# A graph network's edge sums: GpSimd instead of VectorE makes the one-hot tiles

## The chip, the cores and the metric

The kernel runs on one core of one Trainium2 chip. The metric is the time on the device in microseconds of one launch. Engines are called TensorE (PE), VectorE (DVE), ScalarE (ACT), GpSimd (POOL) and SyncE (SP, which here only issues DMAs); SBUF is the on-chip memory of 128 partitions, PSUM the accumulation memory ("pb" in the rows).

## The reference

Four graph layers over 6250 nodes of 128 features, each followed by a layer norm of the residual. The 206250 edges are sorted by destination. The change touches the first layer alone:

```
xw  = x @ W                          # 6250 x 128
ew  = edge_attr @ edge_w             # one row of 128 for each edge
msg = xw[src] * ew
out = segment_sum(msg, dst) + b      # each edge's message added to its destination's row
x   = layernorm(x + out)
# layers 1 to 3: the same edges, with weights that depend only on src and dst
```

## The kernel before

At the start TensorE makes xw and SP stores it to a table in HBM ("xw"). Then comes a loop, unrolled, of NH = 202 steps, one for each 1024 edges (8 tiles of 128 edges, one edge in each partition; the last step has 4 tiles, so 1612 tiles in all). In a step n

- GpSimd issues one indirect DMA for each tile (line 722), which fetches the 128 rows xw[src] into `gath`, a ring of NG = 4 steps. A ring slot is free when the products of step n-4 are done (`s_msg`, line 716). Before the fifth gather of a step (from step 7 on) GpSimd waits for TensorE too (line 721's event): `s_pe >= n`, which is window n-2 done, and `s_amm >= 2 (n-6)`, the dense-adjacency products of step n-2 done. In 25 of the steps it issues one more indirect DMA for the slots of a pair of node blocks (line 705).
- TensorE has made the edge products ew (line 1326) in two PSUM banks; VectorE multiplies them with the gathered rows into `msg` (two instructions, line 909).
- VectorE makes `hot_win`, eight one-hot tiles of 128 edges x 64 nodes in one instruction (line 802, 128 x 512): element (edge, j) is 1 where the edge's destination, counted from the step's first destination, is j. It makes them one step ahead, those of step n+1 in step n; two sets take turns.
- TensorE makes the edge products of step n+1 and then sums the eight tiles' msg^T x hot_win in PSUM (line 1405, the "window"). VectorE adds the window to the sums yT in the following step (line 849).
- Beside this, the step builds a dense adjacency piece for the later layers: one-hot tiles on VectorE (lines 835 and 837), products on TensorE (line 1378), evicted by ScalarE (line 1636), stored by SP (line 618), summed for degrees (line 1384). A "job" of the first layers' norm or of the second layer's sums follows (line 1368 and others).

After the loop the other layers run on dense adjacency chunks read back from HBM; GpSimd has no gathers there. The order on each engine is that of the program; semaphores are the only link. The names in the rows: `big` is the SBUF room that holds gath, msg, hot_win, rel and more; `pb` is PSUM; `tmp` holds the staging tiles. `cols` (columns' numbers) lies in PSUM, `cols_pf` holds the same numbers in SBUF; `rel` is each edge's destination relative to its step's first.

Of the kernel before, what the change touches and what calls it, by code (L numbers as in the profile page):

```python
# [16 lines left out]
ALU = mybir.AluOpType  # L17
# [7 lines left out]
P = 128  # L25
NB = -(-N // P)
NP = NB * P
T8 = 8
SN = 32
NH = 2 * max(-(-E // (2 * T8 * P)), NP // (2 * SN) + 1)  # L30
NI = NH // 2
T = NH * T8
WIN = 64
# [14 lines left out]
LAG = 5  # L48
# [81 lines left out]
def build(nc, xT_d, x_d, ea_d, src_d, dst_d, next_d, edges_d, firstq_d, first16_d, half_d, w_d, vec_d, out_d):  # L130
    ctx = ExitStack()
    with ctx:
# [40 lines left out]
        hot_win = part([P, 2 * T8, WIN], F32)  # L173
# [9 lines left out]
        rel = part([P, T], F32)  # L183
# [70 lines left out]
        cols_pf = sb("cols_pf", [P, P])  # L254
# [17 lines left out]
        cols = PB[:, 7, 0:P + KW]  # L272

        s_in = {n: sem("in_" + n) for n in ("w0", "w", "edge_w", "xT0", "xT1", "xT2", "xT3", "vecs", "src", "edges", "firsts", "rows", "x")}
        s_const = sem("consts_made")
        s_rowxw, s_rowev = sem("xw_mm"), sem("xw_evac")
        s_rowst = [sem(f"xw_stored{h}") for h in range(4)]
        s_tab = sem("dve_table_step")
# [10 lines left out]
        s_seen = sem("wait_over")  # L289
        s_ea = [sem(f"ea_in{h}") for h in range(NG)]  # L290
        s_pe = sem("window_and_next_ew_done")
        s_msg = sem("msg_done")
        s_hotw = sem("hot_win_done")
        s_add = sem("yT_added")
        s_hot = sem("hot_ready")
        s_amm = sem("a_mm")
# [379 lines left out]
        def _(pool):  # L676
# [21 lines left out]
            def slots_in(b):  # L698
                if b == 0:
                    pool.wait_ge(s_firstin, 16)  # L700
                    pool.sem_inc(s_seen, 1)
                if b >= 2:
                    pool.wait_ge(s_prep, b - 1)
                    pool.sem_inc(s_seen, 1)
                nc.gpsimd.indirect_dma_start(slots[:, b % 2, :, :].rearrange("p e k -> p (e k)"), None, edges_d,
                                             bass.IndirectOffsetOnAxis(ap=first_edge[:, b:b + 1], axis=0)).then_inc(s_slot[b % 2], 16)

            pool.wait_ge(s_in["src"], 16)
            pool.wait_ge(s_rowxw, 2 * NT)
            for h in range(4):  # L710
# [2 lines left out]
            for n in range(NH):  # L713
                if n >= NG:
                    pool.wait_ge(s_msg, 2 * (n - NG) + 2)
                    pool.sem_inc(s_seen, 1)
                for t in range(n * T8, min(n * T8 + T8, ET)):
                    if t % T8 == T8 // 2 and n >= LAG + 2:
                        pool.wait_ge(s_pe, n)
                        pool.wait_ge(s_amm, 2 * (n - LAG - 1))  # L720
                        pool.sem_inc(s_seen, 1)
                    nc.gpsimd.indirect_dma_start(gath[:, T8 * (n % NG) + t % T8, :], None, xw_d,  # L722
                                                 bass.IndirectOffsetOnAxis(ap=src_i[:, t:t + 1], axis=0)).then_inc(s_gath[n % NG], 16)
                if n == 0:
                    slots_in(0)
                if n % BL == BL // 2 and n // BL + 1 < NPB:
                    slots_in(n // BL + 1)
            for q in range(NCH):
                here = y[:, CB * q:min(CB * q + CB, NB), :]
                pool.wait_ge(s_w2["xs"], q + 1)  # L730
                nc.gpsimd.tensor_tensor(here, here, vecs[:, B_L2, :].unsqueeze(1).broadcast_to([P, min(CB, NB - CB * q), D]), ALU.add).then_inc(s_w2["yb"], 1)
# [12 lines left out]
            for q in range(NCH - 1):  # L744
# [3 lines left out]
                for h in range(0, CB, 2):  # L748
                    last = nc.gpsimd.tensor_tensor(off_pivot[:, h:h + 2, :], rows_q[:, h:h + 2, :], x[:, 0:2, :], ALU.subtract)  # L749
# [18 lines left out]
        def _(v):  # L768
# [27 lines left out]
            nc.vector.tensor_copy(cols[:, 0:P], cols_pf[:, :])  # L796
            nc.vector.tensor_copy(cols[:, P:P + KW], cols_key[:, :]).then_inc(s_tab, 1)
            v.wait_ge(s_tab, 4)

            def window_hot(n):  # L800
                at_tile = T8 * (n % 2)
                nc.vector.tensor_tensor(hot_win[:, at_tile:at_tile + T8, :], cols[:, 0:WIN].unsqueeze(1).broadcast_to([P, T8, WIN]),  # L802
                                        rel[:, n * T8:n * T8 + T8].unsqueeze(2).broadcast_to([P, T8, WIN]), ALU.is_equal).then_inc(s_hotw, 1)

            cuts = [NPB + 1]

# [94 lines left out]
                    v.wait_ge(s_fhi, g + 1)  # L901
                    nc.vector.scalar_tensor_tensor(out=group(parts_v[1], g), in0=xn_g, scalar=SCALE, in1=group(parts_v[0], g), op0=ALU.mult, op1=ALU.subtract).then_inc(s_part, 1)

            window_hot(0)
            for n in range(NH):
                v.wait_ge(s_pe, n + 1)
                v.wait_ge(s_gath[n % NG], 16 * T8 * (n // NG) + 16 * min(T8, ET - n * T8))
                for q in range(2):
                    nc.vector.tensor_tensor(msg[:, T8 * (n % 2) + 4 * q:T8 * (n % 2) + 4 * q + 4, :], PB[:, q, :].rearrange("p (t f) -> p t f", f=D),  # L909
                                            gath[:, T8 * (n % NG) + 4 * q:T8 * (n % NG) + 4 * q + 4, :], ALU.mult).then_inc(s_msg, 1)  # L910
                if n + 1 < NH:
                    window_hot(n + 1)
                if n > 0:
                    window_add(n - 1)
                job_out(n - 2)
                fold_shift(n)
                if n % BL == 2 and n // BL < NPB:
                    split_slots(n // BL)
                if 0 <= n + 1 - LAG < NA:
                    hots(n + 1 - LAG)  # L920
                fold_stats(n)
                if n == 5:
                    for g in range(NG1):
                        nc.vector.tensor_scalar(flags[:, 3 + g:4 + g], half_i[:, STEP_OF[g]:STEP_OF[g] + 1], float(GB * P * (g + 1)), None, ALU.is_lt)
                        here = win_tab[0:1, STEP_OF[g]:STEP_OF[g + 1] if g + 1 < NG1 else NH]
                        last = nc.vector.tensor_scalar(here, here, float(GB * P * (g + 1)), None, ALU.max)
                    last.then_inc(s_off, 1)
                elif n == 6:
                    v.wait_ge(s_in["rows"], 16)
                    nc.vector.tensor_tensor(less, next_i, dst_i, ALU.is_lt).then_inc(s_off, 1)  # L930
                elif n == 7:
                    v.wait_ge(s_off, 2)
                    nc.vector.tensor_scalar(less, less, 0.0, None, ALU.is_gt, ALU.add, accum_out=flags[:, 1:2]).then_inc(s_off, 1)
                elif n == 8:
                    v.wait_ge(s_off, 3)
                    nc.vector.scalar_tensor_tensor(out=less, in0=dst_i, scalar=float(N), in1=rel[:, 0:T], op0=ALU.is_lt, op1=ALU.mult).then_inc(s_off, 1)
                elif n == 9:
                    v.wait_ge(s_off, 4)
                    nc.vector.tensor_scalar(less, less, float(WIN), None, ALU.is_ge, ALU.add, accum_out=flags[:, 0:1]).then_inc(s_off, 1)
                elif n == BL * (NPB - 1) + 4:  # L940
                    nc.vector.tensor_tensor(pair_deg[:, :, :], below[:, :, 1:3], below[:, :, 0:2], ALU.subtract).then_inc(s_deg["pairs"], 1)
                    nc.vector.tensor_scalar(unused[:, 0, 0:NPB], below[:, :, 2], float(P), None, ALU.is_ge, ALU.add, accum_out=flags[:, 2:3]).then_inc(s_off, 1)
# [6 lines left out]
            for b in range(NL):  # L949
                last = nc.vector.bn_stats(stats[:, 1, b, :], x[:, LB + b, :])  # L950
            last.then_inc(s_lx, 1)
            v.wait_ge(s_lx, 2)
            for b in range(NL):
                last = nc.vector.bn_aggr(mean_var[:, LB + b, :], stats[:, 1, b, :])
# [133 lines left out]
            with v.If(g_off > 0):  # L1088
# [5 lines left out]
                for t in range(NT):  # L1094
# [4 lines left out]
                    for q, nb in ((0, 4), (1, BT - 4)):  # L1099
                        last = nc.vector.tensor_copy(xnT[:, 4 * q:4 * q + nb, :], PB[:, 2 + q, 0:nb * P].rearrange("p (b f) -> p b f", f=D))  # L1100
# [4 lines left out]
                    for q, nb in ((0, 4), (1, BT - 4)):  # L1105
                        last = nc.vector.tensor_tensor(x[:, t * BT + 4 * q:t * BT + 4 * q + nb, :], xn[0][:, 4 * q:4 * q + nb, :], PB[:, 4 + q, 0:nb * P].rearrange("p (b f) -> p b f", f=D), ALU.add)
# [22 lines left out]
            for j in range(NCH):  # L1129
                nb, here = width(j), slice(CB * j, min(CB * j + CB, NB))  # L1130
                v.wait_ge(S["lin"], j + 1)
                for b in range(nb):
                    row = y[:, CB * j + b, :]
                    last = nc.vector.scalar_tensor_tensor(out=row, in0=PB[:, 4 + j % 2, b * P:b * P + P], scalar=on_l2[:, CB * j + b:CB * j + b + 1], in1=row, op0=ALU.mult, op1=ALU.add)
                last.then_inc(S["y"], 1)
                v.wait_ge(S["y"], j + 1)
                for b in range(nb):
                    last = nc.vector.bn_stats(stats[:, j % 2, b, :], y[:, CB * j + b, :])
                last.then_inc(S["stats"], 1)
                v.wait_ge(S["stats"], 2 * j + 1)  # L1140
                for b in range(nb):
                    last = nc.vector.bn_aggr(mean_var[:, CB * j + b, :], stats[:, j % 2, b, :])
# [101 lines left out]
            for h, rows_of in enumerate((low_rows[:, :], float(NB // 2))):  # L1244
                last = nc.vector.scalar_tensor_tensor(out=lane_rows[:, h, :], in0=x[:, h, :], scalar=rows_of, in1=sum_1[:, h, :], op0=ALU.mult, op1=ALU.add)
# [6 lines left out]
            for h, rows_of in enumerate((low_rows[:, :], float(NB // 2))):  # L1252
                last = nc.vector.scalar_tensor_tensor(out=twice_1[:, h, :], in0=lane_rows[:, h, :], scalar=rows_of, in1=twice_1[:, h, :], op0=ALU.mult, op1=ALU.subtract)
# [19 lines left out]
            for t in range(NT + 2):  # L1273
# [4 lines left out]
                if 1 <= t <= NT:  # L1278
                    v.wait_ge(s_bn_sum, t)
                    for b in range(BT):  # L1280
                        last = nc.vector.bn_stats(stats[:, t % 2, b, :], x[:, (t - 1) * BT + b, :])
# [4 lines left out]
                if t < NT:  # L1286
# [5 lines left out]
                    for q, (b0, b1) in enumerate(((0, 4), (4, BT))):  # L1292
                        here = x[:, t * BT + b0:t * BT + b1, :]
                        last = nc.vector.tensor_tensor(here, here, PB[:, 2 + 2 * (t % 3) + q, 0:(b1 - b0) * D].rearrange("p (b f) -> p b f", f=D), ALU.add)
                    last.then_inc(s_bn_sum, 1)
                if 1 <= t <= NT:
                    v.wait_ge(s_bn, stats_at)
                    for b in range(BT):
                        last = nc.vector.bn_aggr(mean_var[:, (t - 1) * BT + b, :], stats[:, t % 2, b, :])
                    aggr_at.append(bn_at(last))  # L1300
            v.wait_ge(s_bn, shift_at[NT - 1])
            for b in range(NB - BT, NB):
                last = nc.vector.tensor_scalar(x[:, b, :], x[:, b, :], rstd[:, b:b + 1], shift[:, b:b + 1], ALU.mult, ALU.add)
# [578 lines left out]
```

## Time and profile before

| | |
|---|---|
| time, median of 3 runs | 2831.36 us (2830.82 to 2834.81) |
| profiled execution, its span | 3281.4 us |
| the page gives no other time of the profiled execution | |
| busy in the span: PE, DVE, POOL, ACT | 2326.1, 1559.3, 1652.8, 497.8 us |
| first and last gather of the loop start at | 32.38 and 2520.00 us |
| gathers in the loop (lines 722 and 705) | 1612 + 25 |

The span is from the first to the last instruction of one profiled execution; it is 450 us longer than the median of the runs that were timed without a profile. In the rows, "idle before <-X" is the time that the engine stood still ahead of an instruction and what ended it; "issue" means that nothing the profile shows was waited for, "remote" that the releaser could not be named. A gather's duration on GpSimd is the time to write its descriptors, not the transfer.

### The profile page before, as it was taken

Reading aid. Unit: us, or ns where it says so; the run is one execution under the profiler, and the core shown is the slowest. Engines: PE = TensorE matmul, PEld = TensorE weight load, DVE = VectorE, ACT = ScalarE, POOL = GpSimd, SP = SyncE. Lnnn points to the kernel's source line nnn. Section 1 sums busy time; section 2 is a strip of 40 time slices with the busy share of each in tenths; the row PEclk is TensorE's granted clock in tenths of the full one; section 3 lists DMA queues with packets and bytes.
Section 4 is the critical chain, followed back from the end, with each engine's and each line's share of the span. In section 5 each row is a group of like instructions: output and inputs, shape, how many; then the busy total and the mean of one; then the engine's idle time right before and its main releaser. Section 6 shows DMA issues by size and latency. Waiting matters only on the chain.

```text
span 3281.4 us, 35388 instructions
## 1 busy us (share of the span) xinstructions
PE 2326.1 (71%) x13074; PEld 1466.3 (45%) x13074; DVE 1559.3 (48%) x2576; ACT 497.8 (15%) x798; POOL 1652.8 (50%) x1762
## 2 busy tenths in 40 slices
PE   3566656666666666667666567666677989999996
PEld 2344444444444444444444344444444544455553
DVE  2555554555554555555555555555554531222126
ACT  1011111111111111111111111111111221111113
POOL 5566656656666666656666656656664110002212
PEclk6556556566666776777777777777777999999998
DMA  6223232323333343433344344444445988876661
GB/s 203 57 86 87 82 88 84 106 84 92 107 96 99 101 122 95 120 100 110 113 135 114 106 116 121 136 121 132 119 128 120 245 294 306 291 268 247 248 242 40
DMA packets 456700, 456.22 MB, mean 139 GB/s; under 512 B 163573, under 2 KB 402250, under 8 KB 456522
## 3 DMA queue, kind: packets, MB, share of 16 engines
q1 hardware_dynamic: 237358, 281.24, 25.7%
q0 software_dynamic: 52832, 109.16, 12.5%
q10 hardware_dynamic: 166332, 63.48, 8.0%
q8 instruction: 108, 1.77, 0.2%
q14 instruction: 70, 0.57, 0.1%
HBM read 368.61 MB, written 85.13 MB: 138 GB/s over the span
## 4 chain that ended last, share of the span: by engine, by line
another core or an unknown queue 46%; PE 35%; ACT 7%; issue 7%; DVE 2%; DMA 2%; SPq 0%; ACTq 0%; POOL 0%; DVEq 0%; POOLq 0%
PE pb L1509 8%; PE pb L1510 8%; ACT tmp L1636 7%; PE pb L1378 5%; PE pb L1405 4%; PE pb L1368 2%; PE pb L1384 2%; PE pb L1326 2%; PE pb L1437 2%; PE pb L1527 1%; DMA big<-at 1%; DMA tmp<-at 0%; ACTq L1642 0%; ACT big L1670 0%
## 5 line engine op out<-in xcount | busy, mean ns | idle before, releaser
L722 POOL DMA_INDIRECT big<-xw,big x1612 | 1527.1, 947 | 954.7 <-issue 580.0
L909 DVE TENSOR_TENSOR big<-pb,big 128x512 f32<-128x512 f32 x404 | 260.0, 685 | 1073.1 <-remote 683.2
L1378 PE MATMUL pb<-big 128*128 128x98 f16 x3136 | 272.9, 248 | 643.2 <-ACT tmp L1636 562.1
L1405 PEld LDWEIGHTS pb<-big 128*128 128x128 f32 x3232 | 546.2, 258 | 349.1 <-issue 334.1
L1405 PE MATMUL pb<-big 128*128 128x64 f32 x3232 | 584.1, 346 | 124.4 <-issue 119.6
L1636 ACT CAST tmp<-pb 128x784 f16<-128x784 f32 x392 | 318.3, 812 | 2043.0 <-remote 1628.5
L1378 PEld LDWEIGHTS pb<-big 128*128 128x128 f16 x3136 | 231.9, 124 | 726.5 <-issue 405.6
L835 DVE TENSOR_TENSOR big<-pb,big 128x2048 f16<-128x2048 f32 x196 | 447.5, 2283 | 0.8
L1326 PE MATMUL pb<-big 64*128 64x512 f32 x808 | 327.3, 898 | 108.4 <-DVE big L909 83.7
L837 DVE TENSOR_TENSOR big<-pb,big 128x1568 f16<-128x1568 f32 x196 | 348.8, 1780 | 0.0
L1384 PE MATMUL pb<-tmp,ident 128*128 128x392 f16 x784 | 239.1, 446 | 0.0
L1509 PE MATMUL pb<-big,x 128*128 128x512 f16 (+1 forms) x637 | 230.3, 369 | 6.6 <-issue 6.6
L1509 PE MATMUL pb<-big,yT 128*128 128x512 f16 (+1 forms) x637 | 230.7, 369 | 3.6 <-DMA big<-at 3.6
L1510 PE MATMUL pb<-big,yT 128*128 128x512 f16 (+1 forms) x637 | 230.5, 369 | 0.0
L1510 PE MATMUL pb<-big,x 128*128 128x512 f16 (+1 forms) x637 | 230.1, 369 | 0.0
L1368 PE MATMUL pb<-big,yT 128*128 128x448 f16 x804 | 199.3, 399 | 9.2 <-issue 9.0
L1326 PEld LDWEIGHTS pb<-big 64*128 64x128 f32 x808 | 83.6, 253 | 135.2 <-DVE big L909 90.2
L749 POOL TENSOR_TENSOR wts<-x 128x256 f32<-128x256 f32 x24 | 16.9, 724 | 246.9 <-DVE x L1206 246.9
L1368 PEld LDWEIGHTS pb<-big,yT 128*128 128x128 f16 x804 | 87.9, 110 | 111.2 <-issue 60.0
L802 DVE TENSOR_TENSOR big<-pb,big 128x512 f32<-128x512 f32 x202 | 137.5, 681 | 0.0
L737 POOL MEMSET vecs<- 128x256 f32 x1 | 0.3, 312 | 271.4 <-DVE yT L1153 271.4
L1384 PEld LDWEIGHTS pb<-tmp,ident 128*128 128x128 f16 x784 | 87.6, 126 | 51.5 <-issue 40.2
(231 smaller groups left out, 1600.0 us busy)
## 6 DMA issues: line engine op xcount, KB each, us to landing
at<-tmp SPq DMA_DIRECT2D x196, 392.0 KB
big<-at SPq DMA_DIRECT2D x24, 3200.0 KB, 10.9
big<-at SPq DMA_DIRECT2D x24, 3072.0 KB, 19.7
big<-at ACTq DMA_DIRECT2D x32, 896.0 KB
big<-xw,big POOLq DMA_INDIRECT x1612
big<-in_ea SPq DMA_DIRECT2D x202, 64.0 KB
big<-at SPq DMA_DIRECT2D x13, 896.0 KB
big<-at ACTq DMA_DIRECT2D x24, 336.0 KB
```

The source lines that it names most:

```text
L722: nc.gpsimd.indirect_dma_start(gath[:, T8 * (n % NG) + t % T8, :], None, xw_d, bass.IndirectOffsetOnAxis(ap=src_i[:, t:t + 1], axis=0)).th ...
L835: nc.vector.tensor_tensor(hot_lo[:, at_pair:at_pair + NPR, :], cols[:, 0:P].unsqueeze(1).broadcast_to([P, NPR, P]), lokeyT[:, b % 3, c:c + ...
L837: last = nc.vector.tensor_tensor(hot_key[:, at_pair:at_pair + NPR, :], cols[:, P:P + KW].unsqueeze(1).broadcast_to([P, NPR, KW]), lokeyT[: ...
L909: nc.vector.tensor_tensor(msg[:, T8 * (n % 2) + 4 * q:T8 * (n % 2) + 4 * q + 4, :], PB[:, q, :].rearrange("p (t f) -> p t f", f=D), gath[: ...
L1326: last = nc.tensor.matmul(PB[:, q, :], ea[4 * ED * q:4 * ED * q + 4 * ED, n % NG, :], edge_w[4 * ED * q:4 * ED * q + 4 * ED, 4 * q:4 * q + ...
L1368: nc.tensor.matmul(bank, parts_v[part_of][:, b0 + b, :], a_piece[:, :, b, :], start=(b == 0 and part_of == 0), stop=(b == size - 1 and par ...
L1378: last = nc.tensor.matmul(PB[:, 4 + g, i * KW:i * KW + KW], hot_lo[:, at_pair, :], hot_key[:, at_pair, :], start=True, stop=True)
L1384: last = nc.tensor.matmul(PB[:, 6, 0:NB * T8], ident16[:, :], stage[:, j % 2, :].rearrange("p (h d) -> p h d", d=SN)[:, :, g * T8:g * T8 + ...
L1405: last = nc.tensor.matmul(PB[:, 2 + n % 2, 0:WIN], msg[:, T8 * (n % 2) + t, :], hot_win[:, T8 * (n % 2) + t, :], start=(t == 0), stop=(t = ...
L1509: nc.tensor.matmul(PB[:, c, 0:n], hi[:, b, :], piece, start=(b == 0), stop=False)
L1510: last = nc.tensor.matmul(PB[:, c, 0:n], lo[:, b, :], piece, start=False, stop=(k == 2 and b == NB - 1))
L1636: nc.scalar.copy(stage[:, j % 2, :].rearrange("p (h d) -> p h d", d=SN)[:, :, c:c + 4 * GP].rearrange("p h (k i a) -> p h k i a", k=2, a=2 ...
```

## The change

GpSimd makes the one-hot tiles, eight instructions of 128 x 64 for each step (one for each tile, with the edge's relative destination as a scalar of each partition, and `cols_pf` in SBUF as the numbers), behind the step's gathers. VectorE's instruction of 128 x 512 goes. GpSimd's wait before the fifth gather goes; the new instructions wait for `s_pe >= n`, that is for window n-2, which read the set they overwrite.

```diff
+            def window_hot(n):
+                if n >= 2:
+                    pool.wait_ge(s_pe, n)
+                for t in range(T8):
+                    last = nc.gpsimd.tensor_scalar(hot_win[:, T8 * (n % 2) + t, :], cols_pf[:, 0:WIN], rel[:, n * T8 + t:n * T8 + t + 1], None, ALU.is_equal)
+                last.then_inc(s_hotw, 1)
...
                 for t in range(n * T8, min(n * T8 + T8, ET)):
-                    if t % T8 == T8 // 2 and n >= LAG + 2:
-                        pool.wait_ge(s_pe, n)
-                        pool.wait_ge(s_amm, 2 * (n - LAG - 1))
-                        pool.sem_inc(s_seen, 1)
                     nc.gpsimd.indirect_dma_start(gath[:, T8 * (n % NG) + t % T8, :], None, xw_d,
                                                  bass.IndirectOffsetOnAxis(ap=src_i[:, t:t + 1], axis=0)).then_inc(s_gath[n % NG], 16)
                 if n == 0:
                     slots_in(0)
+                    pool.wait_ge(s_tab, 2)
+                    pool.wait_ge(s_const, 3)
                 if n % BL == BL // 2 and n // BL + 1 < NPB:
                     slots_in(n // BL + 1)
+                window_hot(n)
...
-            def window_hot(n):
-                at_tile = T8 * (n % 2)
-                nc.vector.tensor_tensor(hot_win[:, at_tile:at_tile + T8, :], cols[:, 0:WIN].unsqueeze(1).broadcast_to([P, T8, WIN]),
-                                        rel[:, n * T8:n * T8 + T8].unsqueeze(2).broadcast_to([P, T8, WIN]), ALU.is_equal).then_inc(s_hotw, 1)
...
-            window_hot(0)
             for n in range(NH):
...
-                if n + 1 < NH:
-                    window_hot(n + 1)
```

On GpSimd, in the middle of the loop, two steps stand in the order before as follows (`msg_done` is `s_msg`, `window_and_next_ew_done` is `s_pe`, `a_mm` is `s_amm`; DMA rows are the gathers):

```order
L722 DMA big<-xw,big 128x128 [waits msg_done]
L722 DMA big<-xw,big 128x128 x3
L722 DMA big<-xw,big 128x128 [waits window_and_next_ew_done,a_mm]
L722 DMA big<-xw,big 128x128 x3
L722 DMA big<-xw,big 128x128 [waits msg_done]
L722 DMA big<-xw,big 128x128 x3
```

The same place after the change:

```order
L725 DMA big<-xw,big 128x128 [waits msg_done]
L725 DMA big<-xw,big 128x128 x7
L712 TENSOR_SCALAR big<-cols_pf,big 128x64 [waits window_and_next_ew_done]
L712 TENSOR_SCALAR big<-cols_pf,big 128x64 x7
L725 DMA big<-xw,big 128x128 [waits msg_done]
L725 DMA big<-xw,big 128x128 x7
```

The wait inside the eight gathers is gone, and eight compute instructions stand between one step's gathers and the next step's.

On VectorE, one step of the loop before (the L909 rows are the products with the gathered rows, L802 the one-hot tiles, L849 the window's addition, L835 and L837 the adjacency's one-hot tiles):

```order
L909 TENSOR_TENSOR big<-pb,big 128x512 [waits gathered3,window_and_next_ew_done]
L909 TENSOR_TENSOR big<-pb,big 128x512
L802 TENSOR_TENSOR big<-pb,big 128x512
L844 TENSOR_LOAD big
L844 ISA x2
L849 ISA [waits yT_added,window_and_next_ew_done]
L849 TENSOR_TENSOR yT<-yT,pb 128x64
L835 TENSOR_TENSOR big<-pb,big 128x2048 [waits lokeyT_ready,a_mm]
L837 TENSOR_TENSOR big<-pb,big 128x1568
```

And after the change:

```order
L909 TENSOR_TENSOR big<-pb,big 128x512 [waits gathered3,window_and_next_ew_done]
L909 TENSOR_TENSOR big<-pb,big 128x512
L845 TENSOR_LOAD big
L845 ISA x2
L850 ISA [waits yT_added,window_and_next_ew_done]
L850 TENSOR_TENSOR yT<-yT,pb 128x64
L836 TENSOR_TENSOR big<-pb,big 128x2048 [waits lokeyT_ready,a_mm]
L838 TENSOR_TENSOR big<-pb,big 128x1568
```

One instruction has gone from each step; the rest stands as it stood.

## Rows read from the trace of the kernel before

**Rows 1.** The page: span, and each engine's busy time, share and instructions.

```profile
span 3281.4 us, 35388 instructions
PE 2326.1 (71%) x13074; PEld 1466.3 (45%) x13074; DVE 1559.3 (48%) x2576; ACT 497.8 (15%) x798; POOL 1652.8 (50%) x1762
```

**Rows 2.** Two stretches: from, to, length, engines' busy time (count), PEclk, DMA share, GB/s.

```profile
32.00:2521.00 2489.00, 1605.22 (x9228) 1076.01 (x9229) 1311.58 (x1774) 353.29 (x489) 1550.81 (x1637) 0.69 0.38 107
2521.00:3281.00 760.00, 704.89 (x3744) 375.88 (x3743) 229.58 (x740) 135.95 (x293) 97.58 (x106) 0.96 0.71 238
```

**Rows 3.** GpSimd's order of time at the loop's start: start, duration, instruction, idle before.

```profile
32.38 0.96 POOL L722 DMA_INDIRECT big<-xw,big  x1 [24.59 <-issue]
33.64 0.95 POOL L722 DMA_INDIRECT big<-xw,big  x1 [0.30 <-issue]
```

**Rows 4.** The same at the loop's end: the last two gathers.

```profile
2518.75 0.95 POOL L722 DMA_INDIRECT big<-xw,big  x1 [0.31 <-issue]
2520.00 0.95 POOL L722 DMA_INDIRECT big<-xw,big  x1 [0.30 <-issue]
```

**Rows 5.** GpSimd's groups by form: count, busy us, mean ns, idle before.

```profile
L722 POOL DMA_INDIRECT big<-xw,big x1612 | 1527.1, 947 | 954.7 <-issue 580.0 <-PE pb L1378 266.3 <-remote 95.0
L705 POOL DMA_INDIRECT big<-in_edges,first_edge x25 | 23.7, 948 | 7.6 <-issue 7.6
L749 POOL TENSOR_TENSOR wts<-x 128x256 f32<-128x256 f32 x24 | 16.9, 724 | 246.9 <-DVE x L1206 246.9
L739 POOL TENSOR_SCALAR valid<-valid 128x1 f32<-128x1 f32 x1 | 0.2, 233 | 0.0
L741 POOL TENSOR_SCALAR low_rows<-valid 128x1 f32<-128x1 f32 x1 | 0.2, 218 | 0.1
```

**Rows 6.** GpSimd in order of time, two steps in the middle of the loop.

```profile
1227.20 0.95 POOL L722 DMA_INDIRECT big<-xw,big  x1 [3.33 <-PE pb L1378]
1228.45 0.95 POOL L722 DMA_INDIRECT big<-xw,big  x1 [0.30 <-issue]
...
1235.96 0.95 POOL L722 DMA_INDIRECT big<-xw,big  x1 [0.30 <-issue]
1237.85 0.95 POOL L722 DMA_INDIRECT big<-xw,big  x1 [0.95 <-issue]
```

**Rows 7.** TensorE, then ScalarE, in order of time at that place.

```profile
1231.15 0.52 PE L1378 MATMUL pb<-big 128*128 128x98 f16 x8
1232.17 2.05 PE L1368 MATMUL pb<-big,yT 128*128 128x448 f16 x10
1238.07 0.67 PE L1378 MATMUL pb<-big 128*128 128x98 f16 x8 [3.84 <-ACT tmp L1636]
...
1237.11 0.81 ACT L1636 CAST tmp<-pb 128x784 f16<-128x784 f32 x1 [7.88 <-remote]
```

**Rows 8.** VectorE's groups between 600 and 2300 us, columns as in rows 5.

```profile
L835 DVE TENSOR_TENSOR big<-pb,big 128x2048 f16<-128x2048 f32 x138 | 315.1, 2283 | 0.6
L909 DVE TENSOR_TENSOR big<-pb,big 128x512 f32<-128x512 f32 x274 | 176.4, 686 | 694.2 <-remote 439.0 <-DMA big<-xw,big 157.2 <-PE pb L1405 84.4
L802 DVE TENSOR_TENSOR big<-pb,big 128x512 f32<-128x512 f32 x137 | 93.3, 681 | 0.0
```

**Rows 9.** GpSimd's order of time where it computes, behind the loop.

```profile
2915.47 0.31 POOL L737 MEMSET vecs<- 128x256 f32 x1 [271.38 <-DVE yT L1153]
2915.72 0.31 POOL L738 MEMSET tmp<- 128x256 f32 x1
...
2955.67 1.30 POOL L749 TENSOR_TENSOR wts<-x 128x256 f32<-128x256 f32 x2 [39.14 <-DVE x L1206]
```

**Rows 10.** VectorE's order of time before the loop: the table of relative destinations, the first one-hots.

```profile
26.91 1.83 DVE L791 TENSOR_TENSOR big<-big 128x1616 f32<-128x1616 int32 x1
29.27 0.69 DVE L802 TENSOR_TENSOR big<-pb,big 128x512 f32<-128x512 f32 x1
```

## The prediction

> **What bounds the kernel now.** I read the page's head first: 3281.4 us of span, no engine busy for more than 71% of it, GpSimd for 50% [rows 1]. A mean over such a span hides its stages, so I cut it at the last gather. Up to there (2489 us) GpSimd's gathers take 1551 us and TensorE is busy for 1605 us at a mean granted clock of 0.69, a mix of its two levels 1.2 and 2.4 GHz; behind it (760 us) TensorE is busy for 705 us at 0.96 and GpSimd for 98 [rows 2]. The second stage is TensorE's, and the change doesn't touch it. The question is what bounds the first.
>
> Gathers start 1.25 us apart wherever nothing is waited for, 0.95 us of it busy and 0.30 idle [rows 3, 4, 6]. That pace is the same directly after a pause of 3.33 us (1227.20 to 1228.45) as in the middle of a run [rows 6]. A queue that is drained at a fixed rate would let the first gathers after a pause come faster; so the pace belongs to GpSimd itself. There are 1612 + 25 gathers [rows 5], and 1636 intervals of 1.251 us (0.947 + 0.304) are 2047 us. From the first gather at 32.38 the last could start at 2079; it starts at 2520.00 [rows 3, 4]. So the profiled execution has 441 us of waits on GpSimd's queue. GpSimd's group says the same: 954.7 us idle, less 24.6 before the first and 1611 times 0.304, leaves 440 [rows 3, 5]. By name most of it ends with TensorE's L1378 (266.3 us), or is unnamed [rows 5]; in two steps in the middle it is 3.33 and 0.65 us ahead of the fifth gather, the place of the wait that the change removes [rows 6].
>
> Now the time without a profile: 2831.36, that is 450 us less than the span. TensorE's stage behind the loop is 93% busy and can't give that back (its idle time is 55 us) [rows 2]. The 450 must come out of the loop, and the loop holds 441 us of waits above the pure pace of the gathers. Head 32.4, gathers 2047.6 and the rest from 2521 on, 760.4, make 2840.4, and the kernel takes 2831. So in a timed run GpSimd gathers practically without a pause. I take it that the profile slows what stands behind those waits: TensorE's eight L1378 matmuls end at 1231.67 by the records and ScalarE, which needs them, starts at 1237.11, 5.4 us later, with nothing else shown between [rows 7]. In a timed run that lag is not there, or not so long. **Forecast: the loop is bound by GpSimd's queue**, whose step is (2831.4 - 32.4 - 760.4) / 202 = 10.09 us, against 8 x 1.251 plus 25 x 1.251 / 202 = 10.16.
>
> **The change, part by part.**
>
> *VectorE loses L802*: 202 times 0.681 us [rows 8]. In the loop VectorE is busy 1312 of 2489 us [rows 2], 6.5 us a step against a step of 10.09. It waits for gathers and TensorE, not they for it. Worth nothing to the time (the other end: if the chain ran through VectorE, 138 us; its 694 us of idle ahead of L909 alone between 600 and 2300 us [rows 8] exclude that).
>
> *The mid-step wait goes*: in the profile 441 us of the span at most, less what reappears elsewhere; in a timed run nothing, since the time is already 9 us below the sum without waits (2840.4). What would take its place is the new wait for window n-2. GpSimd meets it after eight gathers rather than four, so it is half a step (5 us) later for the same count, and the part on `s_amm` is dropped. The step itself becomes 12.3 us (below), and window n-2 is wanted only a full step after its one-hots were made. I count 0 in a timed run and 0 to 40 us in the profile. Behind this wait stand the next step's gathers, and VectorE's products behind these.
>
> *GpSimd gains 202 x 8 = 1616 instructions of 128 x 64.* No row shows one. From below: the element rate of a memset, 256 elements in 0.25 us from start to start [rows 9], gives 0.06 us for 64. From above: a tensor_tensor of 256 elements with two inputs, 1.30 us for two, so 0.58 from start to start [rows 9]; one input and a quarter of the elements can hardly take more. Nearest: tensor_scalar of one element, 0.233 for a comparison and 0.218 for an addition [rows 5]. To 0.22 come 63 elements at about 1 ns (0.06), and from start to start a memset shows 0.06 less than its duration (0.31 against 0.25 [rows 9]): 0.22 to 0.23. The scalar here is read from SBUF for each partition, where those rows had a constant; I add 0.045 for that and take 0.27. Eight: 2.16 us. The passage from gather to compute and back may cost up to the 0.30 idle that each gather has ahead of it, or hide it; I take 0.04. **2.2 us a step, 444 us in 202 steps.** The bounds are 8 x 0.06 x 202 = 97 and (8 x 0.58 + 0.30) x 202 = 998.
>
> By the Trainium skill (GPSIMD Engine Reference, "Performance pitfalls for Q7 kernels" and "Performance versus the Vector engine") each small read command costs about 102 cycles at 1.2 GHz, not overlapped, and a one-input body 1.03 to 2.03 cycles an element. Two reads (tile and scalar) and 64 elements would be 0.22 to 0.28 us, an estimate from that page, and the time 3195 to 3284. No row here has the same instruction; the one-element rows lie beside it. The skill also warns (Perfetto Trace Analysis, on GpSimd's boundaries) that a GpSimd span should be timed from start to start, as is done above. And it rules that elementwise work belongs on VectorE, since GpSimd dispatches in software: one instruction of 0.68 us there against eight here is that rule in numbers.
>
> None of this lies beside other work: GpSimd's queue is in order, and gathers of step n+1 stand behind the one-hots of step n. The slot wait (`s_msg`) allows gathers four steps ahead, so there is always a gather ready to be issued, and each 2.2 us is 2.2 us lost to them.
>
> *Start*: rel is written at 28.74 and VectorE's first one-hots start at 29.27 [rows 10], before the first gather at 32.38 [rows 3]: the two new waits of step 0 cost nothing.
>
> **Sum.** Profiled: 3281.4 - 441 + 444 = 3285, the same as before within its doubt. Timed: the waits are not in the median, so 2831.4 + 444 = **3275 us**. TensorE has room: 1605 us at 0.69 of full clock is 7.9 us a step, and if all of it ran at the lower level (0.5) it would be 11.0, below the new step of 12.3 [rows 2].
>
> **The rivals.**
>
> *A. The gathers are faster without a profile, and the loop is bound by TensorE's chain through the mid-step wait.* Then the 0.30 idle is the profiler's, eight gathers take 7.6 us, and the one-hots fit into a step of 10.09: 7.6 + 2.2 = 9.8. With the wait gone GpSimd runs ahead, gathered rows are never late, and the step falls to that 9.8: 202 x 0.29 = 59 us, 2772 us. It decides at a gather pace of (10.09 - 2.2) / 8 = 0.99 us; below it the change is faster, at 1.05 us it costs 0.5 x 202 = 101 us and gives 2930. For it: the profile's slowness has to come from somewhere, and instructions that report are candidates. Against it: the pace without waits meets the timed loop to 0.07 us a step, which would be chance; and memsets follow each other without any idle time [rows 9]. I give faster 5%, and up to 3100 by a faster gather pace 6% more.
>
> *B. The one-hots are cheap*, 0.15 us or less each, because the cores that don't write descriptors work ahead and only the dispatch counts: 1.2 us a step, 242 us, 3074. Against it the 0.22 of one element [rows 5]. 6%.
>
> *C. They are dear*, 0.45 us or more each: the read of the scalar, the comparison or a stop at each passage from descriptor work to compute. 3.9 us a step, 788 us, 3619. For it: tensor_tensor's 0.58 [rows 9]; against it, the one-element rows. 10%.
>
> *D. TensorE becomes a second bound*: with longer steps it idles more, its clock is granted at the lower level throughout, and in steps with the longest jobs it needs more than 12.3 us. Its mean of 11.0 leaves 1.3 us; if a third of the steps overran by 1.5 us, 100 us more, 3375. 8%, inside the range.
>
> *E. The change does not move the time at all*, the gathers being limited by something that drains behind GpSimd so that one-hots hide in its idle time: 2831. The pace after a pause speaks against it. 3%.
>
> **How the numbers follow.** The forecast with its sizes between 0.19 and 0.42 us an instruction (1.5 to 3.4 us a step, 3140 to 3520) has 62%; D 8%; A 11%; B 6%; C 10%; E 3%. Range 3110 to 3520: it leaves out A and E, most of B and nearly all of C, about 2 in 10. What a measurement of this kernel can tell from no change is about 0.2%, 6 us. Faster 5% (A), same 3% (E), slower 92%.
>
> **What the profile after would show.** Right: a span near 3280, about the same as before, while the time is 400 us longer; start to start of the new instructions near 0.27; GpSimd's idle ahead of gathers near 0.30 each with few waits named; some 12.3 us from one step's first gather to the next. Wrong, if gathers or one-hots wait for TensorE as long as before, if the instruction takes 0.1 or 0.5, or if the time moves by less than 150 us, which would say that a timed gather is shorter than a profiled one.

## The result and the profile after

| | before | after |
|---|---|---|
| time, median | 2832.74 us (4 runs) | 3496.78 us (4 runs) |
| ratio to before | 1 | 1.2339 (95% interval 1.2322 to 1.2357) |
| span of the profiled execution | 3281.4 us | 3493.1 us |

The change costs 664 us, 3.29 us for each of the 202 steps. The forecast was 444 us, 2.2 us a step; the time lies inside the range (3110 to 3520), near its upper end. Ratios and their intervals, here and below, are estimated from the runs of both kernels; the quotient of two medians differs from them by about 0.001.

The page after, its span and busy times, which answer to [rows 1]:

```profile
span 3493.1 us, 36609 instructions
PE 2530.8 (72%) x13074; PEld 1638.9 (47%) x13074; DVE 1443.4 (41%) x2374; ACT 498.4 (14%) x798; POOL 2342.9 (67%) x3378
```

GpSimd has 1616 instructions and 690 us of busy time more, VectorE 202 instructions and 116 us less (202 times 0.68 would be 138; where the other 22 us went is not traced, and nothing below depends on it). The two stages, cut at the last instruction of the loop's queue, answer to [rows 2] (columns as there):

```profile
32.00:2746.00 2714.00, 1819.37 (x9297) 1252.94 (x9298) 1199.45 (x1578) 356.56 (x493) 2238.08 (x3247) 0.65 0.34 98
2746.00:3493.00 747.00, 693.96 (x3677) 370.15 (x3674) 226.49 (x734) 133.29 (x290) 100.08 (x113) 0.97 0.72 242
```

The profiled execution that [rows 2] show was itself 450 us longer than the kernel's time, so its loop can't be set against this one. A second profile of the kernel before (the last experiment below) has a span of 2829.5 us, which fits the time. Its two stages:

```profile
32.00:2080.00 2048.00, 1566.02 (x9252) 1080.00 (x9253) 1316.11 (x1779) 355.43 (x491) 1548.10 (x1637) 0.73 0.46 130
2080.00:2829.00 749.00, 697.34 (x3722) 372.48 (x3720) 226.27 (x734) 134.29 (x291) 97.46 (x106) 0.97 0.72 241
```

The second stage is what it was (749 and 747 us). The first grew from 2048 to 2714 us, by 666: all of the loss is there. GpSimd's groups by form, which answer to [rows 5]:

```profile
L725 POOL DMA_INDIRECT big<-xw,big x1612 | 1542.0, 957 | 485.5 <-issue 485.5
L712 POOL TENSOR_SCALAR big<-cols_pf,big 128x64 f32<-128x64 f32 x1616 | 675.4, 437 | 6.6
L705 POOL DMA_INDIRECT big<-in_edges,first_edge x25 | 23.6, 946 | 7.6 <-issue 7.6
```

All of the gathers' idle time is now "issue": no wait is named. (24 of the 485.5 us stand before the first gather.) The one-hots take 0.437 us each and 675 us in all by their durations, about the 664 us of the result; neighbours overlap a little, so the sum of durations is slightly too high. One step of GpSimd in order of time, in the middle of the loop (start, duration, instruction, idle before), beside [rows 6]:

```profile
1203.07 0.94 POOL L725 DMA_INDIRECT big<-xw,big  x1 [0.30 <-issue]
1204.05 3.34 POOL L712 TENSOR_SCALAR big<-cols_pf,big 128x64 f32<-128x64 f32 x8
1207.55 1.03 POOL L725 DMA_INDIRECT big<-xw,big  x1 [0.16 <-issue]
1208.89 0.94 POOL L725 DMA_INDIRECT big<-xw,big  x1 [0.30 <-issue]
...
1217.34 3.34 POOL L712 TENSOR_SCALAR big<-cols_pf,big 128x64 f32<-128x64 f32 x8
```

From block to block it is 13.29 us. From the start of the eighth gather to that of the next step's first it is 4.48 us instead of 1.25, and the second gather follows 1.34 us behind the first instead of 1.25, because the first takes 1.03 us there and not 0.94: 3.3 us in all for the block. What the other engines do meanwhile shows in the waits (waiter, releaser, us in total, times, longest):

```profile
ACT tmp L1634 <- PE pb L1376: 2262.7, 373, 26.6
DVE big L909 <- DMA big<-xw,big: 1476.4, 201, 18.7
PEld pb L1324 <- DVE big L909: 926.4, 195, 19.9
POOL big L725 <- issue: 485.5, 1612, 23.9
```

VectorE waits for the gathers' data in 201 of 202 steps, 7.3 us a step; TensorE waits for VectorE, ScalarE for TensorE. In the loop GpSimd names no wait for another engine. The chain of waits that ended last says it in one line: POOL 64% of the span, 44% in L725 and 19% in L712.

The one-hots take as long beside a busy VectorE as beside an idle one. The last of each block of eight took 0.433 us in the mean in the 147 steps in which VectorE computed throughout, and 0.430 us in 33 steps in which it stood still. So their price is not a contest with VectorE.

### The profile page after: what moved, and what is told of

Same layout as the page of the kernel before. It is cut to its first block, busy times and chain, and to the rows that moved or that the text cites. A ratio compares the mean times of both kernels' runs of the same rounds, so it can differ in the third digit from the quotient of the medians.

```text
span 3493.1 us, 36609 instructions
## 1 busy us (share of the span) xinstructions
PE 2530.8 (72%) x13074; PEld 1638.9 (47%) x13074; DVE 1443.4 (41%) x2374; ACT 498.4 (14%) x798; POOL 2342.9 (67%) x3378
## 4 chain that ended last, share of the span: by engine, by line
POOL 64%; PE 18%; issue 14%; DMA 2%; DVE 1%; SPq 0%; ACT 0%; POOLq 0%; ACTq 0%; DVEq 0%
POOL big L725 44%; POOL big L712 19%; PE pb L1507 7%; PE pb L1508 7%; PE pb L1435 1%; DMA big<-at 1%; POOL big L705 1%; PE pb L1525 1%; DMA tmp<-at 0%; PE pb L1542 0%; PE pb L1558 0%; DMA xw<-big 0%; DVE stats L1279 0%; DVE x L1292 0%; PE pb L1446 0%
## 5 line engine op out<-in xcount | busy, mean ns | idle before, releaser
L725 POOL DMA_INDIRECT big<-xw,big x1612 | 1542.0, 957 | 485.5 <-issue 485.5
L1324 PE MATMUL pb<-big 64*128 64x512 f32 x808 | 374.3, 1020 | 894.1 <-DVE big L909 891.4
L909 DVE TENSOR_TENSOR big<-pb,big 128x512 f32<-128x512 f32 x404 | 260.3, 686 | 1477.7 <-DMA big<-xw,big 1476.4
L1403 PEld LDWEIGHTS pb<-big 128*128 128x128 f32 x3232 | 663.5, 313 | 272.3 <-issue 236.2
L1403 PE MATMUL pb<-big 128*128 128x64 f32 x3232 | 700.4, 406 | 3.5 <-DVE big L909 2.4
L712 POOL TENSOR_SCALAR big<-cols_pf,big 128x64 f32<-128x64 f32 x1616 | 675.4, 437 | 6.6
L1376 PEld LDWEIGHTS pb<-big 128*128 128x128 f16 x3136 | 276.0, 135 | 40.3 <-issue 18.0
L1376 PE MATMUL pb<-big 128*128 128x98 f16 x3136 | 289.7, 256 | 3.4 <-DVE big L838 2.3
L1382 PE MATMUL pb<-tmp,ident 128*128 128x392 f16 x784 | 280.6, 510 | 0.0
L1382 PEld LDWEIGHTS pb<-tmp,ident 128*128 128x128 f16 x784 | 99.6, 143 | 64.7 <-issue 61.9
```

The lines of the kernel that those rows point to most:

```text
L712: last = nc.gpsimd.tensor_scalar(hot_win[:, T8 * (n % 2) + t, :], cols_pf[:, 0:WIN], rel[:, n * T8 + t:n * T8 + t + 1], None, ALU.is_equal)
L1324: last = nc.tensor.matmul(PB[:, q, :], ea[4 * ED * q:4 * ED * q + 4 * ED, n % NG, :], edge_w[4 * ED * q:4 * ED * q + 4 * ED, 4 * q:4 * q + ...
L1376: last = nc.tensor.matmul(PB[:, 4 + g, i * KW:i * KW + KW], hot_lo[:, at_pair, :], hot_key[:, at_pair, :], start=True, stop=True)
L1382: last = nc.tensor.matmul(PB[:, 6, 0:NB * T8], ident16[:, :], stage[:, j % 2, :].rearrange("p (h d) -> p h d", d=SN)[:, :, g * T8:g * T8 + ...
L1403: last = nc.tensor.matmul(PB[:, 2 + n % 2, 0:WIN], msg[:, T8 * (n % 2) + t, :], hot_win[:, T8 * (n % 2) + t, :], start=(t == 0), stop=(t = ...
```

## The experiments

The theory: the loop lasts as long as GpSimd's in-order queue, a gather is 1.25 us of it, and each one-hot instruction adds its own time. Each experiment's expectation names the rivals that it tells apart. Five of them don't compute the layer's sums, since they leave out gathers, all or half of the one-hots, or the scalar that the one-hots compare with; they tell only of the time.

### The wait alone removed

```diff
-                    if t % T8 == T8 // 2 and n >= LAG + 2:
-                        pool.wait_ge(s_pe, n)
-                        pool.wait_ge(s_amm, 2 * (n - LAG - 1))
-                        pool.sem_inc(s_seen, 1)
```

> Only GpSimd's mid-step wait is removed; VectorE keeps the one-hots. Theory (GpSimd's queue is saturated in a timed run and the wait costs nothing there): time 2832 us within 0.3%, while the profiled span falls from 3281 to about 2840, since the 441 us of waits were the profile's. Rival (the wait holds the timed loop back, gathers being faster than 1.25 us without a profile): the time falls by 1% or more, below 2805.

Measured: 2833.51 us, ratio 1.0001 (0.9991 to 1.0010); span 2830.9. Of GpSimd's waits in that profile, the gathers' is this; two more rows name VectorE, 16 times, for at most 0.3 us each:

```profile
POOL big L718 <- issue: 510.6, 1596, 24.5
```

The wait costs nothing. The last gather starts at 2077.96 us, where the sum of pure gathers had put it (2079). The interval excludes the rival's gain of 1%.

### The one-hots alone moved

The changed kernel with the four lines above put back.

> Only the one-hots are moved to GpSimd; the mid-step wait stays. Theory: the time is that of the full change, 3497 us within 0.3%, because with a step of 13.3 us TensorE is always ahead of the wait. Rival (the wait's removal gave something back in the full change): slower than 3497 by 20 us or more.

Measured: 3497.86 us, ratio to before 1.2346 (1.2326 to 1.2367), the change's own being 1.2339. The removed wait gives nothing back; the whole cost is the one-hots'.

### One gather of eight left out

```diff
-                for t in range(n * T8, min(n * T8 + T8, ET)):
+                for t in [t for t in range(n * T8, min(n * T8 + T8, ET)) if t % T8 not in (6,)]:
...
-                v.wait_ge(s_gath[n % NG], 16 * T8 * (n // NG) + 16 * min(T8, ET - n * T8))
+                v.wait_ge(s_gath[n % NG], 16 * 7 * (n // NG) + 16 * min(7, ET - n * T8))
```

> The kernel before, but the seventh of a step's eight gathers is left out (201 gathers fewer, the products use what lies in the buffer). Theory: each gather is 1.25 us of the time, so 201 x 1.251 = 251 us less, 2581 us, if TensorE's and VectorE's chain allows a step of 8.8 us. Rival (a step of 10.09 us is TensorE's chain, gathers are hidden): 2832 within 1%. Rival (a timed gather is 1.0 us): 2632.

Measured: 2584.16 us, ratio 0.9124 (0.9109 to 0.9139), so 248 us less by the ratio and 251 by the medians, for 201 gathers: 1.23 to 1.25 us each. This is the price of one gather measured in timed runs, and it is the pace of the profile. The 0.30 us of idle ahead of each gather is real time, not the profiler's.

### Three gathers of eight left out

The same edit with `(1, 5, 6)`, and 5 in place of 7 (3 in the last step).

> The kernel before with the second, sixth and seventh gathers of each step left out (604 fewer). It shows the bound that lies under GpSimd's. Theory: GpSimd's queue alone would give 2832 - 604 x 1.251 = 2076 us; I expect the chain through TensorE and VectorE (7 to 9 us a step) to end first, so 2250 to 2600. Rival (TensorE already bounds a step of 10.09): 2832 within 1%.

Measured: 2190.81 us, ratio 0.7741 (0.7721 to 0.7760). Below the range I had written: the chain under GpSimd's bound is faster than I took it for. The loop's stretch, and GpSimd's longest named wait in it:

```profile
32.00:1426.00 1394.00, 1226.86 (x9210) 853.23 (x9210) 1295.20 (x1768) 354.62 (x490) 975.37 (x1033) 0.90 0.57 162
```

```profile
POOL big L722 <- PE pb L1378: 133.0, 106, 6.2
```

A step is 1394 / 202 = 6.9 us, and the mid-step wait on L1378 now does bite (133 us, 0.3 us of idle ahead of each of the 106 gathers included). VectorE is busy for 1295 of the 1394 us (93%). That doesn't make it the next bound: GpSimd's 1033 gathers, 1.25 us apart, fill 1291 us (93%) as well. The two aren't told apart here, and whether taking 0.68 us a step off VectorE would pay at this pace wasn't tried. TensorE was busy for 1227 us at a granted clock of 0.90, where nearly the same matmuls (9210 and 9297 in the two stretches) took it 1819 us at 0.65 in the changed kernel. So its busy time in the changed kernel doesn't say how much time it needs.

### VectorE's relief without its price

The kernel before; the one-hot buffer is zeroed once, VectorE's instruction is left out and nothing comes in its place, so the windows' sums are zeros.

```diff
+            nc.gpsimd.memset(hot_win[:, :, :], 0.0).then_inc(s_hotw, 1)
...
-            window_hot(0)
...
-                if n + 1 < NH:
-                    window_hot(n + 1)
...
-                pe.wait_ge(s_hotw, n + 1)
+                pe.wait_ge(s_hotw, 1)
```

> The kernel before without any one-hot tiles for the windows (their buffer is zeroed once, VectorE's instruction of 128 x 512 goes, nothing is added to GpSimd). It is the change's relief of VectorE without its price. Theory (VectorE is not on the path of the loop): 2833 us within 0.2%. Rival (VectorE's 0.68 us a step is worth something that the change's price covered up): 2700 to 2825 us.

Measured: 2833.53 us, ratio 0.9994 (0.9985 to 1.0004). The relief is worth nothing here.

### A constant for the scalar

```diff
-                    last = nc.gpsimd.tensor_scalar(hot_win[:, T8 * (n % 2) + t, :], cols_pf[:, 0:WIN], rel[:, n * T8 + t:n * T8 + t + 1], None, ALU.is_equal)
+                    last = nc.gpsimd.tensor_scalar(hot_win[:, T8 * (n % 2) + t, :], cols_pf[:, 0:WIN], float(t), None, ALU.is_equal)
```

> The changed kernel with a constant in place of the scalar of each partition (the one-hot tiles hold the wrong columns). Theory S (the read of the scalar made the instruction 0.41 us where 0.27 was forecast): start to start falls to 0.23 to 0.30 and the time by 1616 x 0.11 to 0.18, to 3205 to 3320 us. Theory E (it is the comparison's cost for each element or a fixed cost): start to start stays at 0.41 and the time at 3497.

Measured: 3468.27 us, ratio 1.2236 (1.2216 to 1.2257), 28.5 us less than the change: 0.018 us an instruction. GpSimd's group:

```profile
L712 POOL TENSOR_SCALAR big<-cols_pf 128x64 f32<-128x64 f32 x1616 | 575.2, 373 | 54.8
```

Theory S falls: 0.018, not 0.11 to 0.18. Start to start became uneven (mostly 0.33 to 0.43, 0.39 in the mean), which is why a duration of 0.373 instead of 0.437 bought so little: the idle time ahead of the one-hots rose from 6.6 to 54.8 us, and that ahead of the gathers from 485.5 to 507.7.

### Half of the columns

```diff
-                    last = nc.gpsimd.tensor_scalar(hot_win[:, T8 * (n % 2) + t, :], cols_pf[:, 0:WIN], rel[:, n * T8 + t:n * T8 + t + 1], None, ALU.is_equal)
+                    last = nc.gpsimd.tensor_scalar(hot_win[:, T8 * (n % 2) + t, 0:WIN // 2], cols_pf[:, 0:WIN // 2], rel[:, n * T8 + t:n * T8 + t + 1], None, ALU.is_equal)
...
+            nc.gpsimd.memset(hot_win[:, :, :], 0.0).then_inc(s_const, 1)
```

The other halves are zeroed once ahead of the loop.

> The changed kernel with 32 of 64 columns made by each instruction (the other half stays zero). Theory S (fixed cost with the scalar's read is nearly all, 1 ns an element): start to start 0.38, time about 3445 us. Theory E (the elements cost most, 4 ns or more each): start to start 0.28 or less, time 3285 or less.

Measured: 3368.19 us, ratio 1.1882 (1.1862 to 1.1902), 128.6 us less than the change. Two blocks in order of time:

```profile
1199.96 2.70 POOL L712 TENSOR_SCALAR big<-cols_pf,big 128x32 f32<-128x32 f32 x8
1202.82 1.03 POOL L726 DMA_INDIRECT big<-xw,big  x1 [0.16 <-issue]
...
1212.61 2.70 POOL L712 TENSOR_SCALAR big<-cols_pf,big 128x32 f32<-128x32 f32 x8
```

128.6 / (1616 x 32) = 2.5 ns an element, and the blocks agree: (3.34 - 2.70) / (8 x 32) = 2.5 ns. It lies between my two theories (1 ns and 4 ns). If the cost is a straight line through these two sizes, an instruction of 64 columns is 0.16 us of elements and 0.25 us of fixed cost; a third size wasn't tried.

### Four of eight on GpSimd

VectorE makes tiles 4 to 7 in one instruction of 128 x 256, one step ahead, with a semaphore of its own; GpSimd's loop runs over `range(T8 // 2)`.

> Four of the eight one-hot tiles on GpSimd, the other four on VectorE in one instruction. Theory (cost in proportion to the number of instructions, nothing for the passage): half of the 664 us, 3165 us. Rival (a fixed cost for going from gathers to compute and back): above 3200.

Measured: 3171.04 us, ratio 1.1190 (1.1172 to 1.1209). 336.6 us over the kernel before (2834.47 beside it) for four tiles a step, 1.67 us a step against 3.29 for eight. Four more are 1.62, so 0.405 us a tile, and 0.05 us is left for the passage. This is the theory with a small passage cost; the rival (above 3200) falls.

```profile
1204.50 1.70 POOL L713 TENSOR_SCALAR big<-cols_pf,big 128x64 f32<-128x64 f32 x4
1206.36 1.03 POOL L726 DMA_INDIRECT big<-xw,big  x1 [0.16 <-issue]
```

### One-hots between the gathers

Each one-hot instruction stands right behind its own gather; the wait for window n-2 stands ahead of the step's first gather.

> The changed kernel with each one-hot instruction right behind its own gather instead of all eight behind the eighth. Theory (GpSimd works its queue in order, each instruction costs its own time wherever it stands): 3497 us within 1%. Rival (the 0.30 us of idle ahead of each gather can hide part of a compute instruction, so that eight passages hide more than one): 3497 - 202 x 7 x 0.14 = 3300 us, if each passage saves what the one shows (0.16 idle instead of 0.30). Rival (a passage costs): above 3600.

Measured: 3562.58 us, ratio 1.2571 (1.2550 to 1.2592), 65.8 us over the change; 1.9% over, so outside my 1%, and between the theory and the rival in which a passage costs (above 3600).

```profile
1199.83 1.03 POOL L725 DMA_INDIRECT big<-xw,big  x1 [0.17 <-issue]
1200.89 0.47 POOL L727 TENSOR_SCALAR big<-cols_pf,big 128x64 f32<-128x64 f32 x1
1201.53 1.03 POOL L725 DMA_INDIRECT big<-xw,big  x1 [0.17 <-issue]
```

From gather to gather it is 1.70 us. The idle time shrinks from 0.30 to 0.17 as the first rival had it, but the gather takes 1.03 instead of 0.94 and the one-hot 0.47 instead of 0.43, without the overlap that one-hots in a row have. 65.8 / (202 x 7) = 0.047 us for each passage more: the same 0.05 as from the four tiles. Gathers in a row and computations in a row are the cheaper order.

### The kernel before, profiled once more

> The kernel before, unchanged, profiled once more. Theory P1 (the profile slows TensorE's semaphores whenever GpSimd waits in the middle of a step): the span is 3281 us again, or near it. Theory P2 (the first profiled execution was a slow one by itself; the kernel with the one-hots moved and the wait kept has a span equal to its time): the span is about 2832 us and the last gather ends near 2080 us.

Measured: one run, 2831.32 us; span 2829.5. The page of this profile, and GpSimd at the place of [rows 6] and at the end of the gathers:

```profile
span 2829.5 us, 35388 instructions
PE 2280.3 (81%) x13074; PEld 1467.4 (52%) x13074; DVE 1560.5 (55%) x2576; ACT 498.3 (18%) x798; POOL 1650.1 (58%) x1762
```

```profile
1231.23 0.94 POOL L722 DMA_INDIRECT big<-xw,big  x1 [0.30 <-issue]
1232.48 0.95 POOL L722 DMA_INDIRECT big<-xw,big  x1 [0.30 <-PE pb L1378]
1233.73 0.94 POOL L722 DMA_INDIRECT big<-xw,big  x1 [0.30 <-issue]
...
2077.77 0.94 POOL L722 DMA_INDIRECT big<-xw,big  x1 [0.30 <-issue]
```

The span now equals the time, and the waits ahead of the fifth gather are gone:

```profile
POOL big L722 <- issue: 479.7, 1497, 23.7
POOL big L722 <- PE pb L1378: 16.2, 53, 0.3
```

53 waits of at most 0.3 us, which is the idle ahead of any gather. So the 441 us of waits in the first profile belong to that one execution, not to profiling as such. 33 more executions of the kernel before, timed beside the experiments, had spans of 2828.3 to 2837.6 us at clocks of 0.789 to 0.801, against 3281.4 us at 0.752 in the first profile.

## Why the prediction was right, and what it mis-sized

**What bounds the kernel: right.** The step "a timed run gathers practically without a pause" was argued from a coincidence (head, gathers and tail make 2840, the kernel takes 2831; most of the 9 us over is the tail, 760 us in the first profile and 751 behind the last gather in the second). The experiments show it three ways: a gather left out is worth 1.24 us in timed runs, the wait's removal and VectorE's relief are worth nothing (ratios 1.0001 and 0.9994), and a new profile of the kernel before has its last gather at 2077.77.

**Why the span was 450 us longer: half right.** That the 441 us were not in the timed runs was right. That "the profile slows what stands behind those waits" was wrong: five kernels that keep the wait (the one-hots alone, one and three gathers left out, VectorE's relief, the kernel before again) were profiled at spans within 4 us of their times. For one execution TensorE's signals came late (5.4 us at one place [rows 7]) at a mean clock of 0.75 where it is 0.79 in the second profile. Its page puts 46% of the chain that ended last to "another core or an unknown queue", which the second one's page doesn't name at all. What delayed the signals stays open, since it did not come back. The sum for the span (3285) took those waits out and so missed the measured 3493.1 only by the mis-sized term below; the forecast that the span would be "about the same as before" compared it with an execution that doesn't come back.

**The mid-step wait and its successor: right.** 0 was forecast and 0 measured; the new wait on window n-2 never shows in GpSimd's rows.

**VectorE's relief: right**, 0 of 138 us.

**The size of the one-hots: the term that was mis-sized.** It forecast 0.27 us from start to start and 0.04 us for the passage; 0.41 and 0.05 were measured. Term by term:

| term | forecast | measured | by |
|---|---|---|---|
| elements (64) | 0.06 us, from a memset's rate of 1 ns | 0.16 us, 2.5 ns each | half of the columns, as a straight line |
| reading the scalar | 0.045 | 0.018 | constant scalar |
| the rest of the fixed cost | 0.16 (0.22 of the one-element rows less 0.06 of overlap) | 0.23 | what is left of 0.41 |
| sum, start to start | 0.27 | 0.41 | the blocks |

The memset writes and does not read, and its rate of 1 ns was too low for this comparison, which reads. The rows that read were nearer, though none gives 2.5 ns. The pair in [rows 9], 0.58 us for 256 elements, allows at most 2.3 ns, and that only with no fixed cost. Another line of GpSimd in the same trace, which the prediction doesn't use, has two sizes (columns as in [rows 5]):

```profile
L731 POOL TENSOR_TENSOR y<-y,vecs 128x512 f32<-128x512 f32 x12 | 19.4, 1621 | 102.6 <-DVE tmp L1043 102.6
L731 POOL TENSOR_TENSOR y<-y,vecs 128x128 f32<-128x128 f32 x1 | 0.8, 836 | 0.2 <-DVE tmp L1043 0.2
```

By these durations it is (1.621 - 0.836) / 384 = 2.0 ns an element and 0.57 us fixed. Two other lines give less: L749 takes 0.724 us for 256 elements [rows 5] and L756 1.041 us for 512, 1.2 ns an element. With these slopes in place of the memset's, the forecast would have been 0.29 to 0.34 us an instruction, an estimate; part of the miss would have stayed. The overlap was taken from memsets too; here a duration of 0.43 leaves 0.41 from start to start, 0.02 of overlap. 202 x (8 x 0.41 + 0.05) = 673 us, against 664 measured and 444 forecast; with the 0.405 us of the timed runs it is 665.

That the time fell inside the range is owed to its width: the upper end stood for 0.42 us an instruction, and 0.41 came. The forecast itself had a third too little.

The Trainium skill's figures that the prediction weighed (GPSIMD Engine Reference, "Performance pitfalls for Q7 kernels" and "Performance versus the Vector engine") would have given 0.22 to 0.28 us; the runs show 0.41 us, with 2.5 ns (3.0 cycles at the page's 1.2 GHz) an element against its 1.03 to 2.03, and 18 ns for the scalar's read against its 85. The measurement decides. The Trainium skill's warning (Perfetto Trace Analysis, "GPSIMD Engine Instruction") to time GpSimd from start to start is borne out: summed durations give 675 us, 2% over the 664, and with a constant scalar they are 64 ns shorter while the time fell by 18 ns an instruction. The rule of the Trainium skill (GPSIMD Engine Reference, "Performance versus the Vector engine") that elementwise work belongs on VectorE holds here with numbers: 0.68 us there, 3.3 us for the same tiles here.

**The rivals.** A (a faster gather in timed runs) is refuted by the gather left out. B (cheap one-hots) and E (hidden) are refuted by the result. C (0.45 us or more) was nearly the truth; the measured 0.41 lies at the upper end of the forecast's own 0.19 to 0.42. D (TensorE as a second bound) did not come: its clock did fall, from 0.73 in the loop of the second profile before to 0.65, and its busy time rose from 7.8 to 9.0 us a step, but GpSimd names no wait for it in a step of 13.4.

## What to carry to other kernels

An engine that is busy for half of the span can still be the bound of a stage: count the start-to-start pace of its in-order queue, idle included, and set the sum of the stages against the timed runs, not against one profiled execution. Work moved onto GpSimd's full queue cost its whole start-to-start time here, and work taken off a waiting VectorE was worth nothing. Price a small instruction from a row that reads and writes as it does, with the slope and the fixed cost apart; a memset's rate was 2.5 times too low for this comparison.

## What was not expected of the hardware

- A GpSimd tensor_scalar on 128 x 64 f32 takes 0.41 us from start to start: 2.5 ns an element and 0.25 us fixed (a straight line through 32 and 64 columns), of which the scalar of each partition is 0.018. It didn't matter whether VectorE was busy beside it (0.433 and 0.430 us).
- Each change from gathers to computation and back costs about 0.05 us (0.047 and 0.045 by two experiments). The gather behind a computation has 0.16 of idle ahead of it instead of 0.30, but takes 1.03 instead of 0.94 us; the first one-hot behind a gather takes 0.46 to 0.47 instead of 0.43 and lacks the overlap of 0.02.
- Nearly the same matmuls (9210 and 9297) kept TensorE busy for 1227 us in a loop of 1394 us and for 1819 us in a loop of 2714 us; the granted clock was 0.90 and 0.65. In these runs a TensorE that was held up more was granted less, and its busy time grew without any more work: the mean clock was 0.92, 0.84, 0.79, 0.75 and 0.72 at spans of 2187, 2580, 2830, 3167 and 3493 us.
- One profiled execution of the kernel before was 450 us longer than its timed runs, at a clock of 0.75; a second was not, at 0.79. Of the added time 440 us were idle time ahead of GpSimd's gathers, of which 266 end with TensorE's L1378 by name; the cause is open.
